# Graph network kernel, layers 1 and 3: the last column of nine blocks is fetched row by row by SyncE

## The reference

```python
h = relu(layernorm(x)); x = x + L0(h)   # sum, max, mean of edge attributes by src; MLP
h = relu(layernorm(x)); x = x + L1(h)   # graph attention, 8 heads:
    logits = leaky_relu(a_src[src] + a_dst[dst])       # softmax over the edges of dst
    out = segment_sum(h[src] * alpha, dst)
h = relu(layernorm(x)); x = x + L2(h)   # silu of edge, sender and receiver parts, mean by dst
h = relu(layernorm(x)); x = x + L3(h)   # with Wh = h @ W + b:
    sim = cos(Wh[row], Wh[col])
    out = segment_sum(base * sim * Wh[col], row)
```

## Time and profile before

| | |
|---|---|
| time, median of 3 runs | 3093.05 us |
| lowest and highest | 3091.59 and 3096.49 us |
| span of the profiled execution | 3095.7 us |
| layer 1 gather on POOL | 841.6 to 1392.6 us |
| layer 3 gather on POOL | 2483.6 to 3033.6 us |
| POOL busy | 2190.4 us, 71% |
| DVE busy | 1326.6 us, 43% |
| granted TensorE clock, mean | 0.577 |

### The profile page before, as it was taken

The page is one execution under the profiler, slowest core; times in us unless marked ns, Lnnn a source line. Parts: engine busy times, 40 slices in busy tenths (PEclk is TensorE's granted clock), DMA queues, the critical chain, the costliest instruction groups (busy, mean ns, idle before and its releaser), DMA issues.

```text
span 3095.7 us, 14532 instructions
## 1 busy us (share of the span) xinstructions
PE 610.1 (20%) x3300; PEld 466.1 (15%) x3301; DVE 1326.6 (43%) x1981; ACT 481.9 (16%) x447; POOL 2190.4 (71%) x2299
## 2 busy tenths in 40 slices
PE   5521130001410000001888860000000400000001
PEld 5411110001300000001676640000000300000001
DVE  8888885202310000008466643233244615353455
ACT  2200006211100000000000022223223212111220
POOL 0177777777777777777777777777777377777774
PEclk8665565555555555555899875555555555555555
DMA  9311114212344755645355424323232123223231
GB/s 325 112 25 14 14 27 100 64 34 63 66 52 53 67 57 60 65 52 65 106 135 155 111 50 74 109 91 128 91 109 92 45 56 85 78 72 91 72 90 52
DMA packets 192274, 248.04 MB, mean 80 GB/s; under 512 B 135507, under 2 KB 146381, under 8 KB 184662
## 3 DMA queue, kind: packets, MB, share of 16 engines
q0 software_dynamic: 74048, 114.24, 19.1%
q1 hardware_dynamic: 60102, 103.67, 10.0%
q10 hardware_dynamic: 58064, 29.51, 7.9%
HBM read 154.17 MB, written 93.09 MB: 80 GB/s over the span
## 4 chain that ended last, share of the span: by engine, by line
POOL 55%; issue 19%; DVE 2%; ACT 0%; DMA 0%; DVEq 0%; POOLq 0%; ACTq 0%
POOL l1g_rows L831 13%; POOL l2g_rows L831 13%; POOL l3g_rows L831 12%; POOL ep_rows L1370 11%; POOL ep_rows L1351 2%; POOL l2t_res L2457 1%; POOL l3t_res L2866 1%; POOL l0f_res L1008 1%; DVE l3g_banks L2813 0%; DVE l3g_banks L2837 0%; ACT l3g_banks L2771 0%; DVE l3g_banks L2834 0%; DVE l3g_dot L2820 0%; DVEq L2819 0%; POOL ep_rows L1379 0%
## 5 line engine op out<-in xcount | busy, mean ns | idle before, releaser
L878 POOL DMA_INDIRECT l0g_rows<-in_rec_s,ents x440 | 427.4, 971 | 137.6 <-issue 133.9
L831 POOL DMA_INDIRECT l2g_rows<-tab,ep_rows x440 | 416.8, 947 | 134.2 <-issue 134.2
L831 POOL DMA_INDIRECT l1g_rows<-tab,srct x440 | 416.8, 947 | 134.2 <-issue 134.2
L831 POOL DMA_INDIRECT l3g_rows<-tab,others x440 | 416.1, 946 | 134.2 <-issue 134.2
L1370 POOL DMA_INDIRECT ep_rows<-recp,entd x352 | 338.7, 962 | 107.3 <-issue 107.3
L1572 DVE TENSOR_TENSOR l1s_A<-l1s_bank,l1s_mk 110x512 f32<-110x512 f32 x8 | 5.2, 686 | 528.4 <-PE l1s_bank L1534 528.4
L1831 PE MATMUL l1a_pa<-l1a_g,l1a_wt 128*128 x1296 | 169.6, 291 | 0.0
L1831 PEld LDWEIGHTS l1a_pa<-l1a_g,l1a_wt 128*128 128x128 f32 x1296 | 158.9, 202 | 23.8 <-issue 23.8
L2811 DVE COPY l3g_banks<-l3g_q 128x65 f32<-128x65 f32 x12 | 2.7, 229 | 306.8 <-ACT l3g_banks L2771 306.4
L2397 DVE COPY l2g_mix<-l2g_q 128x64 f32<-128x64 f32 x11 | 2.5, 228 | 306.9 <-ACT l2g_mix L2358 306.9
L1534 PE MATMUL l1s_bank<-ident,atp 128*110 128x128 f32 x64 | 10.9, 347 | 539.7 <-ACT atp L1473 530.6
(11 more groups left out here) (582 smaller groups left out, 2330.2 us busy)
## 6 DMA issues: line engine op xcount, KB each, us to landing
l1a_g<-g SPq DMA_DIRECT2D x54, 390.0 KB
recp<-ep_rows ACTq DMA_DIRECT2D x11, 1320.0 KB, 5.9
g<-l1g_rows ACTq DMA_DIRECT2D x10, 1430.0 KB, 22.7
sums<-l0s_sums SPq DMA_DIRECT2D x10, 1408.0 KB, 5.1
sums<-l2o_sums SPq DMA_DIRECT2D x9, 1408.0 KB, 4.9
sums<-l3o_sums SPq DMA_DIRECT2D x9, 1408.0 KB, 5.3
rowsd<-ep_rows POOLq DMA_DIRECT2D x8, 1452.0 KB, 5.9
ep_rows<-rowsd SPq DMA_DIRECT2D x8, 1452.0 KB, 6.6
```

Source lines behind the costliest of these rows:

```text
L831: nc.gpsimd.indirect_dma_start(out=ring.rows[:, s, j, :], out_offset=None, in_=table, in_offset=bass.IndirectOffsetOnAxis(ap=index(b, s, j ...
L878: nc.gpsimd.indirect_dma_start(out=rows[:, j, :], out_offset=None, in_=K.a["rec_s"], in_offset=bass.IndirectOffsetOnAxis(ap=K.by_src.ent[: ...
```

## The change

For blocks 0 to 8 of layers 1 and 3, POOL no longer issues the gather of column 43, the last. SP issues it instead as 128 transfers of one row each. It loads eight node numbers at a time from one partition into registers and uses each as the address of a transfer. In layer 1 the numbers come from the list `pairs`, masked by DVE; SP does this work after the list of windows. In layer 3 they are written to HBM and read back as one row during layer 2's tail, and the fetches stand in SP's order ahead of the stores of the packed sums. Those who wait for a block wait for SP's rows too. ACT's loop in `layer1_gather` is written out instead of looped. Block 9 stays with POOL as it was, and so does layer 2.

```diff
+SINGLE = TB - 1
+SINGLES = NBLK - 1
+AT_ONCE = 8
...
+def fetch_rows(K, sp, rows, table, numbers, k, most, landed):
+    for p in range(0, P, AT_ONCE):
+        begins = values(K.nc, numbers[0:1, k * P + p:k * P + p + AT_ONCE], mybir.EngineType.SP, most)
+        for i in range(AT_ONCE):
+            sp.dma_start(rows[p + i:p + i + 1, :], table(begins[i])).then_inc(landed, 16)
...
         for j in range(TB):
+            if b < singles and j == SINGLE:
+                continue
...
-            rounds(act, body)
-    layer1_items(K)
+            for it in range(NBLK // RING):
                 for s in range(RING):
-                    act.wait_ge(ring.gathered[s], ring.base[s] + (it + 1) * TB * 16)
+                    act.wait_ge(ring.gathered[s], ring.base[s] + ((it + 1) * TB - singles(it, s)) * 16)
+                    act.wait_ge(K.l1.single[s], singles(it, s) * P * 16)
...
+def layer1_singles(K):
+            sp.wait_ge(K.l1.numbered, 1)
+            for b in range(SINGLES):
+                s, it = b % RING, b // RING
+                if it:
+                    sp.wait_ge(kept[s], it)
+                    sp.wait_ge(stored[s], it * 16)
+                fetch_rows(K, sp, ring.rows[:, s, SINGLE, :], lambda n: K.tab1[bass.ds(n, 1), :], K.sources, b, NP - 1, K.l1.single[s])
...
 (layer1_items, SP, then DVE)
+                sp.dma_start(K.sources[:, :].rearrange("o (b p) -> o b p", p=P),
+                             K.pairs[0:SINGLES * TB * P].rearrange("(b t p) -> t b p", t=TB, p=P)[SINGLE:SINGLE + 1]).then_inc(K.l1.listed, 16)
                 v.memset(ones[:, :], 1.0)
+                dve.wait_ge(K.l1.listed, 16)
+                v.tensor_scalar(K.sources[:, :], K.sources[:, :], 0xFFF, None, ALU.bitwise_and).then_inc(K.l1.numbered, 1)
...
 (layer2_tail, SP)
+                sp.wait_ge(offset, 2)
+                    sp.dma_start(K.numbersd.rearrange("k p -> p k"), by_src.other[:, SINGLE:SINGLES * TB:TB]).then_inc(listed, 16)
+                sp.wait_ge(listed, 32)
+                sp.dma_start(K.numbers[:, :], K.numbersd.rearrange("k p -> (k p)").unsqueeze(0)).then_inc(listed, 16)
...
 (layer3_gather, SP)
+                def fetch(b):
+                    s, it = b % RING, b // RING
+                    if it:
+                        sp.wait_ge(freed[s], it)
+                    fetch_rows(K, sp, ring.rows[:, s, SINGLE, :], lambda n: entries[bass.ds(n, R3)].unsqueeze(0), K.numbers, b,
+                               NP * R3N - R3, single[s])
+                for b in range(RING):
+                    fetch(b)
                 for i, (b, c0, n, landed, count) in enumerate(parts):
+                    if i and RING + i - 1 < SINGLES:
+                        fetch(RING + i - 1)
                     sp.wait_ge(packed, i + 1)
...
 (layer3_gather, ACT; DVE waits alike behind its wait for landed)
                     act.wait_ge(landed, count)
+                    if i < SINGLES:
+                        act.wait_ge(single[b % RING], (b // RING + 1) * P * 16)
```

More of the change, by code:

```diff
@@ L155, in build @@
         K.tab3 = dram("tab3", (NP * R3N // R3, R3))
+        K.numbersd = dram("numbersd", (SINGLES, P), I32)
         K.tab3n = K.tab3.rearrange("a b -> (a b)").rearrange("(n r) -> n r", r=R3N)
@@ L170, in build @@
                     K.l1 = SourceRows(rows)
-                    layer1_gather(K)
+                    with nc.sbuf_tensor("sources", [1, SINGLES * P], I32) as K.sources:
+                        layer1_gather(K)
+                        layer1_items(K)
+                        layer1_singles(K)
                     layer1_softmax(K)
@@ L179, in build @@
                     layer1_tail(K, T)
-            with nc.sbuf_tensor("wh", [P, NT, R3], F32) as K.wh:
+            with nc.sbuf_tensor("wh", [P, NT, R3], F32) as K.wh, \
+                    nc.sbuf_tensor("numbers", [1, SINGLES * P], I32) as K.numbers:
                 with Phase(K, "l2o") as ph:
@@ L816, in block_cols, with gather_blocks @@
 def block_cols(it, s, size=RING):
-    return bass.ds((it * size + s) * TB, TB)
-def gather_blocks(nc, pool, ring, table, index, ready, last=None, axis=0):
+    return slice((it * size + s) * TB, (it * size + s + 1) * TB)
+def fetch_rows(K, sp, rows, table, numbers, k, most, landed):
[3 more added lines that the diff above has]
+            sp.dma_start(rows[p + i:p + i + 1, :], table(begins[i])).then_inc(landed, 16)
+def gather_blocks(nc, pool, ring, table, index, ready, last=None, axis=0, singles=0):
     for b in range(NBLK):
@@ L834, in gather_blocks, with pieces @@
             ).then_inc(landed, 16)
-def pieces(ring, last):
-    whole = [(b, 0, TB, ring.gathered[b % RING], ring.base[b % RING] + (b // RING + 1) * TB * 16) for b in range(NBLK - 1)]
+def pieces(ring, last, singles=0):
+    whole = [(b, 0, TB, ring.gathered[b % RING], ring.base[b % RING] + (b // RING + 1) * (TB - (b < singles)) * 16) for b in range(NBLK - 1)]
     return whole + [(NBLK - 1, c, n, sem, base + n * 16) for (c, n), (sem, base) in zip(LAST, last)]
@@ L1446, in __init__ @@
         self.stored = [ph.sem(f"stored{s}") for s in range(RING)]
+        self.single = [ph.sem(f"single{s}") for s in range(RING)]
+        self.listed, self.numbered = ph.sems("listed", "numbered")
 def layer1_gather(K):
@@ L1464, in _, with singles @@
             store_edges(K, nc, pool, slice(RING * TB, (RING + 1) * TB), 0, TB * 16)
-            gather_blocks(nc, pool, ring, K.tab1, lambda b, s, j: K.srct[:, b * TB + j:b * TB + j + 1], ready)
+            gather_blocks(nc, pool, ring, K.tab1, lambda b, s, j: K.srct[:, b * TB + j:b * TB + j + 1], ready,
+                          singles=SINGLES)
         @block.scalar
         def _(act):
-            def body(it, first):
+            def singles(it, s):
+                return min(it + 1, len(range(s, SINGLES, RING)))
+            for it in range(NBLK // RING):
                 for s in range(RING):
-                    act.wait_ge(ring.gathered[s], ring.base[s] + (it + 1) * TB * 16)
+                    act.wait_ge(ring.gathered[s], ring.base[s] + ((it + 1) * TB - singles(it, s)) * 16)
+                    act.wait_ge(K.l1.single[s], singles(it, s) * P * 16)
                     act.dma_start(K.g1[:, block_cols(it, s), :], ring.rows[:, s, :, 0:D + 1]).then_inc(stored[s], 16)
                     nc.scalar.copy(K.atp[:, block_cols(it, s), :], ring.rows[:, s, :, D + 1:D + 17]).then_inc(kept[s], 1)
-            rounds(act, body)
-    layer1_items(K)
+def layer1_singles(K):
+    nc = K.nc
+    ring, kept, stored = K.l1.ring, K.l1.kept, K.l1.stored
+    with Step(nc, meet=False) as block:
+        @block.sync
+        def _(sp):
+            sp.wait_ge(K.l1.numbered, 1)
[5 more added lines that the diff above has]
+                fetch_rows(K, sp, ring.rows[:, s, SINGLE, :], lambda n: K.tab1[bass.ds(n, 1), :], K.sources, b, NP - 1, K.l1.single[s])
 def edge_order(K):
@@ L2425, in layer2_tail @@
     nc = K.nc
-    by = K.by_dst
+    by, by_src = K.by_dst, K.by_src
     with Phase(K, "l2t") as ph:
@@ L2447, in layer2_tail @@
         added, summed, tabled, stored = ph.sems("added", "summed", "tabled", "stored")
+        offset, listed = K.l1.numbered, K.l1.listed
         K.tab3_stored = (stored, NG * 16)
@@ L2462, in _ @@
                 rows = lambda t: t.rearrange("(w p) r -> p w r", p=P)
+                sp.wait_ge(offset, 2)
+                with nc.allow_non_contiguous_dma(reason="one column of numbers for each of nine blocks, once"):
+                    sp.dma_start(K.numbersd.rearrange("k p -> p k"), by_src.other[:, SINGLE:SINGLES * TB:TB]).then_inc(listed, 16)
+                sp.wait_ge(listed, 32)
+                sp.dma_start(K.numbers[:, :], K.numbersd.rearrange("k p -> (k p)").unsqueeze(0)).then_inc(listed, 16)
                 for g, (w, n) in enumerate(GROUPS):
@@ L2617, in _ @@
                 v.tensor_tensor(other[:, :], whole[:, 0:J], whole[:, J:2 * J], ALU.add)
-                v.drain()
+                v.drain().then_inc(offset, 1)
                 wide = lambda c, ws, n: c[:, ws].unsqueeze(2).to_broadcast([P, n, D])
@@ L2727, in layer3_gather @@
         last = [ph.gather_sem(f"last{i}") for i in range(len(LAST))]
-        freed = [ph.sem(f"freed{s}") for s in range(RING)]
+        freed, single = ([ph.sem(f"{n}{s}") for s in range(RING)] for n in ("freed", "single"))
         out = K.sums3.rearrange("(p j) d -> p j d", p=P)
-        parts = pieces(ring, last)
+        parts = pieces(ring, last, SINGLES)
         def cut(t, f, n):
@@ L2746, in ready @@
                         pool.wait_ge(freed[s], it)
-                gather_blocks(nc, pool, ring, K.tab3, lambda b, s, j: K.by_src.other[:, b * TB + j:b * TB + j + 1], ready, last, axis=1)
+                gather_blocks(nc, pool, ring, K.tab3, lambda b, s, j: K.by_src.other[:, b * TB + j:b * TB + j + 1], ready, last, axis=1, singles=SINGLES)
             @block.sync
             def _(sp):
+                entries = K.tab3.rearrange("a b -> (a b)")
```

(10 more changed lines are left out.)

## The result

The changed kernel takes 3319.12 us (median of 4 runs, 3317.03 to 3323.09) against 3094.28 us: 1.073 of before, with a 95% interval of 1.071 to 1.074. That is 225 us slower; 304 were forecast. The profiled execution spans 3321.3 us, 225.6 more than before.

What follows compares the result with a forecast made beforehand. POOL, busy 71% of the span, was taken as the bound; SP, at 73.0 us per block against POOL's 53.8, would replace it. Layer 1's +142 and layer 3's +161, together +304 on the 3093 median, gave 3397 us, range 3206 to 3640.

Steps and rivals of the forecast that it cites:

- X: SP's fetches in layers 1 and 3: issuing one single-row transfer takes 300 ns; each 10 ns is worth 21.8 us.
- the 212 of the line drawn through the larger transfers: SP's one-row issue, estimate from below: a line from 319 ns at 128 rows to 256 at 53 reaches 212.
- The load of eight values: SP's register load per 8 rows: 636 ns, with a gap 0.676 us, x 16 = 10.8 us per block.
- Rival (4): SP's issue held up by others' traffic, layer 1's eight ACT stores adding 182 us: 3579 us; chance 0.09.
- a sign for this: SP's block in the profile after: longer than 128 (X + 186) + 10.8 us means SP waits, Rival (4) or Rival (5).
- Layer 1: SP's fetches pace the gather; POOL ends at 1534.7 against 1392.6, +142 us.
- Layer 2's tail: Writing and loading layer 3's numbers before SP's first table store has some 45 us of cover, costed at nothing.
- Layer 3: SP's rows of block 8 are there at 3141.5 against 2980.1, +161 us; the tail moves whole.
- Rival (1): SP keeps up in layers 1 and 3: faster from X = 160 ns, at best 3070.5 us; chance 0.07.
- Rival (5): Fetched rows go one behind another on one DMA engine, 2.0 us or more each: 6500 us; chance 0.05.
- Rival (2): SP's issue cheap but not enough, X of 160 to 246: 3100 to 3280 us, say 3206; chance 0.16.
- rival (3): The forecast itself: SP bound with X of 246 to 411, 3280 to 3639 us; chance 0.61.

Runs made afterwards that it cites:

- run 1: Changed kernel with the same one-row transfers from fixed addresses, no register loads or address arithmetic: 3082.1 us, 0.995 of before.
- run 2: Changed kernel with SP fetching 96 of 128 rows one by one, the other 32 in one transfer of fixed rows: 3077.6 us, 0.994 of before.
- run 9: Changed kernel with ACT's store of layer 1's block 8 put off until block 9 has landed: 3316.77 us, against 3325.53 for the changed kernel.
- run 5: Changed kernel with both gathers back on POOL; layer 3's numbers still written and read in layer 2's tail, unused: 3103.84 us against 3096.1 before.
- run 7: Changed kernel with SP fetching rows 0 to 95 of each column and ACT rows 96 to 127: 3081.12 us, 0.995 of before.
- run 8: As run 7, with layer 3's numbers written and read at the start of layer 2's gather: 3076.77 us, 0.994 of before.

## Why the prediction was right

**The bound.** The forecast's mechanism holds: SP's block is longer than POOL's in both layers, POOL waits, and the delay passes whole to what follows. Runs 1 and 2 exclude that the transfers, the shared engine or the waits cost it. By blocks the account closes: SP's pace of 69.2 us instead of 73.0 in layer 1, with its earlier start and a quicker landing of the store, makes POOL's end 36 us less late than forecast; 66.6 instead of 73.0 in layer 3 takes off 58; the late landing (11) and layer 2's tail (6) come on top: 304 - 36 - 58 + 11 + 6 = 227, where 225 were measured. Inside a block these terms of the sum had other sizes than forecast:

- **X, the issue of one row.** 300 ns forecast, 225 measured in layer 1 and 228 in layer 3. At 21.8 us per 10 ns, 75 ns are 163 us. It lies between the 212 of the line drawn through the larger transfers and the 246 of the least row. I went up from these because of L2300's 411 ns, the only transfer of a single row, and that was the misjudged step: single rows one right behind the other took 248 to 252 ns in run 1. Why L2300 took 411 stays open. By the rows the fewer-rows line alone would have been 13 ns low. The work around it was right in layer 1: 37, 29 and gaps, 184 ns, where 186 was taken. In layer 3 a row begins with an ALU_OP of 33 ns in place of the FUSED_REGOPS and has shorter gaps: the median from row to row is 392 ns there, 164 beside the issue, which is 25 us less over 1152 rows.
- **The load of eight values.** 636 ns forecast from a line between one and twelve values, 781 measured, on SP, where the row of twelve was TensorE's queue. 0.145 x 16 x 17 = 39 us that the forecast lacked.
- **SP's issues held up.** Rival (4) has a small part in it. Behind ACT's stores some of SP's issues, four or five per store, take 0.5 to 0.9 us. In the stretch from 1422.5 to 1427.2 us of the changed kernel, right behind the store of 1422.00:

```profile
L834 SPq DMA_DIRECT2D l1g_rows<-tab x6: 225/824/925, 1422.6 to 1426.4; - x6
```

against a median of 225 over all. With eight stores at some 2.5 us each that is about 20 us, not the 182 of the rival. The 22.7 us of a store delay SP only in its first 5. In layer 3 fourteen issues are held up, 8 us in all.

The prediction had a sign for this: a block longer than 128 (X + 186) + 10.8 us would mean that SP waits. With X = 225 that is 63.4 us, and layer 1 took 69.2. But the sign was not clean, since of the 5.8 us some 2.3 are the loads' own length (16 x 0.145) and only some 2.5 the held-up issues.

**Layer 1.** +142 forecast, +117 measured at ACT's last copy. Of that 106 is SP's pace (POOL's last gather starts at 1497.17, where the prediction had 1534), and 11 the late landing of run 9, which I hadn't seen: before, the store of block 8 started some 55 us ahead of the last copy (ACT's wait of 54.63) and was long done. Now it starts at 1491.72, 5.5 us before POOL's last gather.

**Layer 2's tail.** Nothing forecast; the stretch is 6.4 us longer (60.0 against 53.6), and run 5 is 7.7 us slower than before. I looked at what SP waits for and where it is covered, and not at what the small pieces do to POOL's transfers in flight. The chain of that stretch ran through POOL's collection.

**Layer 3.** +161 forecast. ACT turns block 8 at 3205.69; from the layer's start at 2604.5 that is 601.2 us, before 497.8: +103.4. The tail moved whole, as forecast: from that turning to the last store 70.0 us (3205.69 to 3275.71), before 69.6.

```profile
3204.63 0.36 SPq L2819 DMA_DIRECT2D sums<-l3o_sums  x1
...
3205.69 5.49 ACT L2838 COPY l3g_banks<-l3g_rows 128x2860 f32<-128x2860 f32 x1 [31.11 <-DMA l3g_rows<-tab]
...
3275.71 0.32 SPq L2819 DMA_DIRECT2D sums<-l3o_sums  x1
```

**The other side.** Rival (1), faster, asked for a block of 55.1 us or X = 160. Runs 2, 7 and 8 show the threshold from the other side: with 96 rows on SP its block is 53 us on average and the kernel 15 to 20 us faster, close to the 22.5 of that rival. Rival (5) is excluded by run 1, where a row took 290 to 294 ns and not 2 us, and by the packets of 21 and 28 ns in the changed kernel. Rival (2) comes nearest to the measured X: 225 lies in its 160 to 246, and by the prediction's formula it gives 3397 - 163 = 3234 us. That the time of 3319 fell into the band of rival (3), X of 246 to 411, is luck: the loads, the held-up issues, the late landing and the tail, which the sum lacked, made up for part of an X that was too high.

## What to carry to other kernels

Before work goes from a busy engine to an idle one, compare the two per block with everything that the second must execute for it: here 392 to 409 ns per row, of which less than 230 is the transfer's issue, and 98 ns per row for the register load. An idle engine that needs 69 us where the busy one needed 54 is the new bound, and a two-slot ring passes its pace on at once. Then give it only as much as fits (96 of 128 rows), and look for what else is in flight when small transfers are added.

## What the runs showed of the hardware

- A one-row transfer costs SP 225 to 228 ns and ACT 235 ns to issue, for 328 as for 520 bytes; a single transfer of 128 rows 319 to 333. At fixed addresses, one right behind the other, 248 to 252.
- Register loads on SP, median: one value 268 to 275 ns, eight 781 to 784, thirty-two 2122 to 2128.
- 1152 pieces of 4 bytes held up the landing of POOL's gathers beside them for about 8 us; a store of 5632 pieces of 260 bytes held up a gather's landing by some 11 to 13 us (14.4 and 15.5 us to ACT's copy in two executions, 2.9 without the store), four or five issues of SP by 0.3 to 0.7 us each, and one issue of ACT behind it by up to 14.6 us.
